# Neighbour sums on padded planes and a root kept in PSUM in the second pass of a two-layer convolution

## The reference, cut to what matters

```python
def reference(x, L0_conv_weights1):        # x: (32, 64, 128, 128) float32
    x = x + _L0_conv_ref(_gn(x), L0_conv_weights1)   # Hartley transform, 20 x 20 modes mixed
    x = x + _L1_conv_ref(_gn(x))                     # layer 1
    return x

def _L1_conv_ref(x):                       # depthwise, 'SAME' padding
    kx = [[-1, 0, 1], [-2, 0, 2], [-1, 0, 1]]
    ky = [[1, 2, 1], [0, 0, 0], [-1, -2, -1]]
    return sqrt(gx * gx + gy * gy + 1e-8)  # gx, gy: x convolved with kx and ky

def _gn(v, G=32, eps=1e-5):                # over pairs of channels of one image
    return (g - mean(g)) / sqrt(var(g) + eps)
```

## Time and profile before

| what | value |
|---|---|
| median of three runs | 2905.59 us (2889.78 to 2907.07) |
| the profiled execution | 2896.12 us, its span 2894.3 us |
| PE busy | 2736.1 us, 95% of the span |
| DVE busy | 2073.9 us, 72% |
| ACT busy | 2096.0 us, 72% |
| POOL busy | 911.3 us, 31% |
| granted TensorE clock over the span | 0.957 |

### The profile page before, as it was taken

How to read it: one execution, slowest core, us unless ns; L and a number is a source line. 1 busy time by engine, 2 the same in 40 slices (tenths; PEclk the granted TensorE clock), 3 DMA queues, 4 the chain that set the end, 5 groups by cost and what they waited for, 6 DMA issues and landing times.

```text
span 2894.3 us, 51534 instructions
## 1 busy us (share of the span) xinstructions
PE 2736.1 (95%) x16764; PEld 2151.0 (74%) x16764; DVE 2073.9 (72%) x2783; ACT 2096.0 (72%) x3633; POOL 911.3 (31%) x533
## 2 busy tenths in 40 slices
PE   6999999999999666899999999999999999999998
PEld 6989889898899666566666666666666666666666
DVE  5767666676777534677877777877777877877777
ACT  5767666576667323578878878878878878888887
POOL 2323233232333302233333333333333333333332
PEclk9999898898999677899999999999999999999999
DMA  6545454454555324155555555555555555555554
GB/s 188 156 133 150 132 146 132 131 155 131 152 144 148 76 62 105 44 150 164 162 152 165 160 150 165 160 156 161 161 153 166 158 152 165 160 153 163 165 167 124
DMA packets 808870, 421.14 MB, mean 146 GB/s; under 512 B 20912, under 2 KB 807344, under 8 KB 807472
## 3 DMA queue, kind: packets, MB, share of 16 engines
q1 hardware_dynamic: 808624, 417.86, 50.7%
HBM read 283.56 MB, written 134.22 MB: 144 GB/s over the span
## 4 chain that ended last, share of the span: by engine, by line
PE 49%; ACT 5%; DVE 3%; issue 3%; DVEq 0%; ACTq 0%
PE g_ps L963 37%; PE y_ps L949 6%; PE v_ps L937 5%; ACT grad L1026 3%; ACT g_ps L1019 2%; DVE coef_t L1063 1%; DVE grad L1075 1%; PE v_ps L925 1%; ACT u_hi L1004 0%; ACT grad L1017 0%; ACT v_sb L1010 0%; DVE xbuf L1100 0%; DVE xbuf L1070 0%; DVE coef L1106 0%; DVEq L1100 0%
## 5 line engine op out<-in xcount | busy, mean ns | idle before, releaser
L963 PE MATMUL g_ps<-u_hi,stencil 128*128 128x512 f32 x2560 | 1054.7, 412 | 1.9 <-DVE grad L1075 1.9
L963 PE MATMUL g_ps<-u_lo,stencil 128*128 128x512 f32 x2560 | 1018.6, 398 | 0.0
L905 POOL TENSOR_TENSOR u_lo<-xbuf,u_hi 128x1024 fp32r<-128x1024 f32 x256 | 565.6, 2209 | 1139.9 <-ACT u_hi L1004 1133.8
L963 PEld LDWEIGHTS g_ps<-u_hi,stencil 128*128 128x128 f32 x2560 | 484.2, 189 | 305.6 <-issue 188.9
L1100 DVE SCALAR_TENSOR_TENSOR xbuf<-xbuf,rows,grad 128x256 f32<-128x256 f32 x1024 | 575.7, 602 | 153.0 <-ACT grad L1026 152.8
L332 PEld LDWEIGHTS t_ps<-first_sb,xbuf 128*128 128x128 f32 x4096 | 525.1, 201 | 68.8 <-issue 42.5
L963 PEld LDWEIGHTS g_ps<-u_lo,stencil 128*128 128x128 f32 x2560 | 482.5, 188 | 103.0
L332 PE MATMUL t_ps<-first_sb,xbuf 128*128 128x64 f32 x4096 | 512.4, 281 | 39.9 <-DMA second_sb<-second 23.5
L1026 ACT ACTIVATE grad<-grad,eps,rows 128x256 f32<-128x256 f32 x1024 | 530.5, 595 | 0.1
L1017 ACT ACTIVATE grad<-g_ps 128x512 f32<-128x512 f32 x512 | 302.2, 590 | 293.1 <-PE g_ps L963 293.0
L1075 DVE TENSOR_TENSOR grad<-grad,g_ps 128x512 f32<-128x512 f32 x512 | 352.0, 687 | 224.6 <-ACT g_ps L1019 218.0
(11 more groups left out here) (116 smaller groups left out, 2383.3 us busy)
## 6 DMA issues: line engine op xcount, KB each, us to landing
xbuf<-x SPq DMA_DIRECT2D x256, 512.0 KB, 5.1
xbuf<-x SPq DMA_DIRECT2D x512, 256.0 KB, 3.0
out<-xbuf SPq DMA_DIRECT2D x512, 256.0 KB, 2.7
xbuf<-weights SPq DMA_DIRECT2D x8, 800.0 KB, 11.2
wmix<-weights SPq DMA_DIRECT2D x8, 800.0 KB, 13.8
second_sb<-second SPq DMA_DIRECT2D x1, 1230.0 KB, 8.4
mats_sb<-mats SPq DMA_DIRECT2D x1, 704.0 KB, 6.5
first_sb<-first SPq DMA_DIRECT2D x1, 32.0 KB, 6.4
```

The source lines that it names most:

```text
L905: nc.gpsimd.tensor_tensor(u_lo[:, r % 2, :, 1:W + 1], x_of(xbuf, r), u_hi[:, r % 2, :, 1:W + 1].bitcast(FP32), ALU.subtract)\
L963: mm = nc.tensor.matmul(g_ps[h][:, axis], stencil[:, m, :], u[:, r % 2, 4 * h:4 * h + 4, o:o + W], start=n == 0, stop=n == len(todo) - 1)
```

## The change

The input buffer gets a second view, `xpad`: eight slots of eight planes, each row of a plane with a zero column on either side (130 columns). The old view, `xbuf`, lies on the same memory and serves the first two stages. With the planes padded:

- POOL `neighbours` computes `pairs`, the sum of each column and the next (129 columns), for step r+2. ACT `high` rounds `pairs` to p_hi, and POOL `low` takes the remainder p_lo from `pairs`. `pairs` has one buffer.
- The filter along the columns is the smoothed difference of two neighbour sums, and the one along the rows the difference of two neighbour sums added. So `sobel` has four taps for each axis and half: 16 a step, for 20 before.
- ACT `squares` puts bank 0's square into `across` in SBUF. DVE `add` writes the sum into bank 1 of g_ps[h], `roots` works in place there, and `finish` reads the root from there. `grad` and `eps` are gone; the root's 1e-8 is a constant of the instruction.
- PE's taps of bank 0 wait for the squares of the step before; those of bank 1 wait for `finished[h]` of the step before. `finished` becomes one semaphore per half, and SP stores a half when it is done.
- The order within a step changes on ACT (roots first, then `high` and `copy_v`) and on DVE (both halves of `finish` before `centre`).

```diff
-        xbuf = sb(keep, "xbuf", [128, SLOTS, CHUNK, W])
+        x_all = sb(keep, "xbuf", [128, XSTEPS * HALF * (W + 2)])
+        xbuf = x_all[:, 0:SLOTS * CHUNK * W].rearrange("p (s n w) -> p s n w", s=SLOTS, w=W)
+
+        xpad = x_all[:].rearrange("p (s n w) -> p s n w", s=XSTEPS, w=W + 2)
...
+
+def x_of(xpad, r):
+
+    return xpad[:, r % XSTEPS, :, 1:W + 1]
...
-        u_hi = sb(ctx, "u_hi", [128, 2, HALF, W + 2], FP32R)
-        u_lo = sb(ctx, "u_lo", [128, 2, HALF, W + 2], FP32R)
-        stencil = sb(ctx, "stencil", [128, 4, 128], FP32R)
-        grad = sb(ctx, "grad", [128, 2, 2, 512])
-        eps = sb(ctx, "eps", [128, 1])
+        pairs = sb(ctx, "pairs", [128, HALF, W + 2])
+        p_hi = sb(ctx, "p_hi", [128, 2, HALF, W + 2], FP32R)
+        p_lo = sb(ctx, "p_lo", [128, 2, HALF, W + 2], FP32R)
+        stencil = sb(ctx, "stencil", [128, 3, 128], FP32R)
+        across = sb(ctx, "across", [128, 2, 512])
...
                 done = sp.snap(t * PSTEPS + r + 1)
-                sp.wait_ge(finished, done)
                 for q in range(2):
-                    sp.dma_start(out_p[:, planes_of(t, r, q), :], x_of(xbuf, r % XSTEPS)[:, 4 * q:4 * q + 4, :])\
+                    sp.wait_ge(finished[q], done)
+                    sp.dma_start(out_p[:, planes_of(t, r, q), :], x_of(xpad, r % XSTEPS)[:, 4 * q:4 * q + 4, :])\
                         .then_inc(stored[r % XSTEPS], 16)
...
-            for part in (u_hi, u_lo):
-                nc.gpsimd.memset(part[:, :, :, 0:W + 2:W + 1].bitcast(FP32), 0.0).then_inc(cleared, 1)
+            nc.gpsimd.memset(xpad[:, :, :, 0:W + 2:W + 1], 0.0).then_inc(padded, 1)
+
+            def neighbours(i, r):
+                pool.wait_ge(centred, at(i, r) + 1)
+                plane = xpad[:, r % XSTEPS]
+                nc.gpsimd.tensor_tensor(pairs[:, :, 0:W + 1], plane[:, :, 0:W + 1], plane[:, :, 1:W + 2],
+                                        ALU.add).then_inc(paired, 1)
 
             def low(i, r):
                 pool.wait_ge(hi_ready, at(i, r) + 1)
-                if not before(i, r, 2):
-                    pool.wait_ge(pe_grad, at(i, r) * 2 - 2)
-                nc.gpsimd.tensor_tensor(u_lo[:, r % 2, :, 1:W + 1], x_of(xbuf, r),
-                                        u_hi[:, r % 2, :, 1:W + 1].bitcast(FP32), ALU.subtract)\
-                    .then_inc(lo_ready, 1)
+                nc.gpsimd.tensor_tensor(p_lo[:, r % 2, :, 0:W + 1], pairs[:, :, 0:W + 1],
+                                        p_hi[:, r % 2, :, 0:W + 1].bitcast(FP32), ALU.subtract).then_inc(lo_ready, 1)
 
             def step(i, r):
                 if not beyond(i, r + 1):
                     low(i, r + 1)
-
+                if not beyond(i, r + 2):
+                    pool.wait_ge(lo_ready, at(i, r) + 2)
+                    neighbours(i, r + 2)
+
+            pool.wait_ge(padded, 1)
+            neighbours(0, 0)
             low(0, 0)
+            pool.wait_ge(lo_ready, 1)
+            neighbours(0, 1)
...
                     pe.wait_ge(lo_ready, at(i, r) + 1)
-                if not before(i, r, 1):
-                    pe.wait_ge(added, at(i, r) * 2 + h - 1)
-
-                SMOOTH, SMOOTH_NEG, DIFF, DIFF_TWICE = range(4)
-                taps = [[(SMOOTH_NEG, 0), (SMOOTH, 2)], [(DIFF, 0), (DIFF_TWICE, 1), (DIFF, 2)]]
+
+                SMOOTH, SMOOTH_NEG, DIFF = range(3)
+                taps = [[(SMOOTH_NEG, 0), (SMOOTH, 1)], [(DIFF, 0), (DIFF, 1)]]
                 for axis in range(2):
-                    todo = [(u, m, o) for m, o in taps[axis] for u in (u_hi, u_lo)]
-                    for n, (u, m, o) in enumerate(todo):
+                    if not before(i, r, 1):
+                        if axis == 0:
+                            pe.wait_ge(squared, at(i, r) * 2 + h - 1)
+                        else:
+                            pe.wait_ge(finished[h], at(i, r))
+                    todo = [(p, m, o) for m, o in taps[axis] for p in (p_hi, p_lo)]
+                    for n, (p, m, o) in enumerate(todo):
                         mm = nc.tensor.matmul(g_ps[h][:, axis], stencil[:, m, :],
-                                              u[:, r % 2, 4 * h:4 * h + 4, o:o + W],
+                                              p[:, r % 2, 4 * h:4 * h + 4, o:o + W],
                                               start=n == 0, stop=n == len(todo) - 1)
                 mm.then_inc(pe_grad, 1)
 
...
             def high(i, r):
-                act.wait_ge(centred, at(i, r) + 1)
+                act.wait_ge(paired, at(i, r) + 1)
                 if not before(i, r, 2):
                     act.wait_ge(pe_grad, at(i, r) * 2 - 2)
-                nc.scalar.activation(u_hi[:, r % 2, :, 1:W + 1], x_of(xbuf, r), ACT.Copy).then_inc(hi_ready, 1)
+                nc.scalar.activation(p_hi[:, r % 2, :, 0:W + 1], pairs[:, :, 0:W + 1], ACT.Copy).then_inc(hi_ready, 1)
...
                 act.wait_ge(pe_grad, at(i, r) * 2 + h + 1)
-                if not before(i, r, 2):
-                    act.wait_ge(finished, at(i, r) - 1)
-                nc.scalar.activation(grad[:, r % 2, h], g_ps[h][:, 0].rearrange("p n w -> p (n w)"), ACT.Square)
-                across = g_ps[h][:, 1].rearrange("p n w -> p (n w)")
-                nc.scalar.activation(across, across, ACT.Square).then_inc(squared, 1)
+                if not before(i, r, 1):
+                    act.wait_ge(added, at(i, r) * 2 + h - 1)
+                nc.scalar.activation(across[:, h], g_ps[h][:, 0].rearrange("p n w -> p (n w)"), ACT.Square)
+                down = g_ps[h][:, 1].rearrange("p n w -> p (n w)")
+                nc.scalar.activation(down, down, ACT.Square).then_inc(squared, 1)
 
             def roots(i, r, h):
                 act.wait_ge(added, at(i, r) * 2 + h + 1)
                 inv_var = rows[:, 0].rearrange("p t n -> p (t n)")
                 for k in range(2):
-                    f = grad[:, r % 2, h, 256 * k:256 * (k + 1)]
-                    a = nc.scalar.activation(f, f, ACT.Sqrt, bias=eps[:],
+                    f = g_ps[h][:, 1, 2 * k:2 * k + 2]
+                    a = nc.scalar.activation(f, f, ACT.Sqrt, bias=EPS_SOBEL,
                                              scale=inv_var[:, bass.ds(group_planes(i, r, h, k), 1)])
                 a.then_inc(rooted, 1)
 
@@ -1038,13 +1053,13 @@
             high(0, 0)
 
             def step(i, r):
+                if not before(i, r, 1):
+                    roots(i, r - 1, 0)
+                    roots(i, r - 1, 1)
                 if not beyond(i, r + 1):
                     high(i, r + 1)
                 if not beyond(i, r + 3):
                     copy_v(i, r + 3)
-                if not before(i, r, 1):
-                    roots(i, r - 1, 0)
-                    roots(i, r - 1, 1)
                 squares(i, r, 0)
                 squares(i, r, 1)
...
-                f = grad[:, r % 2, h]
-                V.tensor_tensor(f, f, g_ps[h][:, 1].rearrange("p n w -> p (n w)"), ALU.add).then_inc(added, 1)
+                down = g_ps[h][:, 1].rearrange("p n w -> p (n w)")
+                V.tensor_tensor(down, across[:, h], down, ALU.add).then_inc(added, 1)
...
                 dve.wait_ge(rooted, at(i, r) * 2 + h + 1)
                 for k in range(2):
-                    xs = x_of(xbuf, r)[:, 4 * h + 2 * k:4 * h + 2 * k + 2, :].rearrange("p n w -> p (n w)")
-                    v = V.scalar_tensor_tensor(
-                        xs, xs, mean[:, bass.ds(group_planes(i, r, h, k), 1)],
-                        grad[:, r % 2, h, 256 * k:256 * (k + 1)], ALU.add, ALU.add)
-                if h == 1:
-                    v.then_inc(finished, 1)
+                    xs = x_of(xpad, r)[:, 4 * h + 2 * k:4 * h + 2 * k + 2, :]
+                    v = V.scalar_tensor_tensor(xs, xs, mean[:, bass.ds(group_planes(i, r, h, k), 1)],
+                                               g_ps[h][:, 1, 2 * k:2 * k + 2], ALU.add, ALU.add)
+                v.then_inc(finished[h], 1)
...
-                V.tensor_copy(stencil[:, n, :], mat(m))
-            V.tensor_scalar(stencil[:, 3, :], mat("diff"), 2.0, None, ALU.mult)
-            V.memset(eps[:], EPS_SOBEL).then_inc(setup, 1)
+                copied = V.tensor_copy(stencil[:, n, :], mat(m))
+            copied.then_inc(setup, 1)
...
                 if not before(i, r, 1):
                     add(i, r - 1, 1)
+                    finish(i, r - 1, 0)
+                    finish(i, r - 1, 1)
                 if not beyond(i, r + 2):
                     centre(i, r + 2)
                 if 1 <= s <= COEF_STEPS and not beyond(i, r - s + PSTEPS):
                     for part in range(4 // COEF_STEPS * (s - 1), 4 // COEF_STEPS * s):
                         for q in range(2):
                             coefficients(pair_of(i, r) + 1, part, q)
-                if not before(i, r, 1):
-                    finish(i, r - 1, 0)
                 add(i, r, 0)
                 if group(i, r) is not None:
```

(2 more changed lines are left out.)

28 lines of the change are left out of this document (13 added, 15 removed).

## The result

| | median us | runs |
|---|---|---|
| before | 2905.59 | 13 |
| changed | 2885.46 | 13 |

The ratio of the two is 0.994, with a 95% interval of 0.9919 to 0.9961. One run on each side was disturbed (5479 and 3795 us): the medians stand over all 13, the ratio leaves the two out. The changed kernel is 20 us faster, a small difference but clear of the noise; 24 us slower was forecast. The profiled execution took 2890.3 us, the one of before 2896.1.

A forecast was written before the change was run, and what follows sets the result against it. TensorE bounds the kernel before; afterwards the loop through the banks should set plain steps. Terms -49 + 69 - 10 + 14 = +24 us on the median 2905.6 gave 2930 us, range 2845 to 2995 (a tenth left out at either end).

The forecast's parts named there:

- the root: ScalarE's square root of 256 elements: 0.48 to 0.50 us, following by 0.40; bounds 0.36 and 0.595 us.
- Taps and bound: Sobel on TensorE, 20 taps to 16: its step falls 0.94 us to 5.48 us and stops being the bound.
- The loop through the banks: Plain step, squares, two roots, two additions, twelve taps: 6.11 us against 6.42, -49 us over 157 intervals.
- The second loop: Through the single buffer `pairs`, remainder, neighbour sum, rounding: 5.8 us, hidden 0.3 us deep.
- The coefficient steps: 28 steps where VectorE and GpSimd take turns, so TENSOR_SCALARs wait: 8.9 us against 6.42, +69 us.
- The clock: TensorE falls to 1.2 GHz once or twice in each of seven coefficient stretches: +14 us, bounds 0 and +50.
- theory (b): Experiments' theory: in coefficient steps VectorE and GpSimd take turns; this delay and the following clock falls take the gain back.
- The transpose steps: 70 steps with fewer taps but a wait for `copy_coef`: 7.0 us against 7.2, -10 us in all.
- Rival 1: Turn taking costs little, coefficient step near 6.4 us, clock stays: -59 us, 2847 us; chance 0.20.
- Rival 2: TensorE's clock does not hold in plain steps either: +105 us on top, 3035 us; chance 0.10.
- Rival 3: Neighbour sum longer than remainder, +125 us, or root keeps 0.595 us, +40, 2970 us; chance 0.20 together.
- a loss of 83 against a gain of 59: Second pass: coefficient steps +69 and clock +14 us against plain steps -49 and transpose steps -10; sum +24 us, slower.

The follow-up runs named there:

- the experiment: Changed kernel with the root's bias read from a column in SBUF again instead of the constant: 2931.5 us, ratio 1.0095 to the kernel before.
- the sums alone: Changed kernel with padded planes, GpSimd neighbour sums and 16 taps kept, but gradient sum and root in SBUF, order and bank release as before: 3076.7 us.
- the banks alone: Kernel before, 20 taps and padding kept, with sum, root and addition in PSUM, constant bias, banks held and new order: 3017.1 us, ratio 1.037.

## Why the prediction was wrong

The order of things was as forecast. What failed are three terms of the sum, all in the same direction: the period of a coefficient step (8.9 us taken, 8.1 measured; in it the neighbour sum, 2.23 against 1.91, and the roots), the root (0.50 taken, 0.443 measured) and the price of the clock's falls (14 us taken, about 2 measured). The measured parts of the pass sum to -25.5 us where mine summed to +24.

**Taps and bound.** Right. TensorE's 5.48 us did not become the bound, and the chain shows what did.

**The loop through the banks.** Right in its order, forecast 6.11 and measured 6.00. The step that failed is the root: 0.48 to 0.50 us taken, following by 0.40, against 0.443 and 0.355. I allowed for the column, which is worth 91 ns by the experiment, but put the move from SBUF to PSUM at nothing for the root, though I had named it as unseen for the addition. It is worth 61 ns a root. Over the 150 plain intervals this and the rest of the pass's plain steps make -16 us of the error (46.5 forecast at 0.31 each, 62.6 measured). The Trainium skill, "ScalarE: Activation LUTs", section "What ACT_TABLE_LOAD costs", has 93 ns for a column, and the trace agrees. The Trainium skill, "Perfetto Trace Analysis", section "Optimizing Scalar/DVE Operations", gives ScalarE some 93 ns of access overhead on SBUF and 51 on PSUM as busy time, 42 apart, and says that a profiled duration holds about twice that; the 61 measured lie between 42 and 84.

**The second loop.** Named rightly as hidden, wrongly priced: the remainder took 2.43 (2.23 taken), the neighbour sum 1.91 (2.23 taken). Two reads of the same tile, one shifted, and a plain fp32 result are not the price of a subtraction rounded to fp32r; that they were was an assumption from "same engine, operation and size".

**The coefficient steps.** The mechanism was the forecast one and decided the case. The four lines of TENSOR_SCALAR average 1.76 to 1.88 us, inside my 1.5 to 2.3. The period was 8.9 and is 8.10. Piece by piece for the step shown above, measured against taken: remainder 2.40 (2.23), gap before the neighbour sum 0.16 (0.23, for the first TENSOR_SCALAR), neighbour sum 1.91 (2.23), rest of the second TENSOR_SCALAR 0.23 (0.23), addition 0.67 (0.69), release 0.14 (0.14), four roots 1.44 (1.70), rounding 1.08 (1.05), release 0.08 (0.17). These sum to 8.1 against 8.7, and I had then gone up to 8.9 for grants that would need the full 0.42 us. The neighbour sum and the roots are 0.58 of it. 28 steps x 0.8 = 22 us of the error: the largest piece.

**The clock.** The falls were forecast rightly, their price was not. The clock held in plain steps and fell one to three times in each of the seven stretches. But the five intervals of a set take 39.1 to 39.2 us in the first, the fourth and the sixth pair, with two, one and one falls in them, and that is just four steps of 8.07 and the first transpose interval, 6.86: the falls cost nothing there. In the second and the seventh pair 0.6 and 1.6 us are left. TensorE is not what these steps wait for, which would explain it; that is argued, not shown. The third and the fifth pair take 4.4 us more each. There the loop is re-entered, and the kernel with the scaling moved takes 4.7 and 4.3 us more in the same places; the kernel before took 1.1 and 0.5. So the falls cost about 2 us, which is -12 of the error; of theory (b) the delay stands and the falls hardly count. The re-entries, which I had not in the sum, are +7. The interval that I counted as plain in each set was a transpose one (eleven a set, 77 and not 70) and gained nothing: +2.

**The transpose steps.** -0.26 us each instead of -0.15, -8 us of the error, and the reason was wrong. The wait for `copy_coef` was not in the loop (the swap of the axes gained nothing). The wait for `copy_v` ahead of the transposes and the transposes themselves were (moving them gained 0.6 us a step). With this the pieces of the error are -16, -22, -12, +7, +2 and -8: together -49, as between +24 and -25.5.

**The rivals.** Rival 1 asked for TENSOR_SCALARs under 0.8 us; they took 1.76 to 1.88, so the turns did cost. Its 2847 would have needed what the moved scaling did, and that gave 2816. The measured 2885 lies halfway between this rival and the forecast, but the mechanism was the forecast's. Rival 2 fell: between 1700 and 1820 us TensorE idled 6.3 of 120 us, a third of a microsecond in each step, and the granted clock was 1.00. The rule of the Trainium skill, "TensorE: Matmul & The Clock Gate", section "A second HAM failure mode: psum-queue depth-cycling", does not show in this kernel's plain steps. Rival 3's root that keeps its column costs +46 us where I had +40, but with a root of 534 ns and not 595. The direction went wrong because I set a loss of 83 against a gain of 59, and the runs gave 55 against 81. The root's size lay inside its bounds, toward the end that I had not taken; the neighbour sum had an upper bound in rival 3 and none below the remainder's own time, and that is what the working lacked.

## What to carry to other kernels

While GpSimd is busy with operations on SBUF, count for VectorE an operation of the kinds below whose tensors all lie in SBUF as waiting for the end of GpSimd's running one, however small it is; put it into the gap in which GpSimd waits, or bring an operand into PSUM. When a buffer's release closes a loop over several engines, only what stands between the release and the loop's last work counts: moving the transposes out of it gained 0.6 us a step without making them shorter, and no busy share shows that. And where a forecast is the small difference of two large terms, price the operations whose memory or inputs change one by one, since their errors can all point one way.

## What the runs showed of the hardware

- VectorE and GpSimd: TENSOR_SCALAR, TENSOR_TENSOR, SCALAR_TENSOR_TENSOR and COPY took turns with GpSimd when all their tensors lay in SBUF (TENSOR_SCALAR 0.42 us unhindered and up to 2.15 in the changed kernel, COPY 0.16 and 1.87, SCALAR_TENSOR_TENSOR 0.44 to 0.48 and up to 2.72 in the sums alone; TENSOR_TENSOR was only seen hindered, 1.67 to 2.40). With the root in PSUM SCALAR_TENSOR_TENSOR did not: all 1024 of L1115 in the changed kernel take 472 to 485 ns. The Trainium skill, "SBUF — State Buffer", section "SBUF: two separate sides", names an exclusive lock between GpSimd and VectorE operations in a two-port mode, or with two SBUF inputs against a GpSimd operation that reads SBUF. These runs agree, with the numbers above; in which mode TENSOR_SCALAR and COPY ran no row shows.
- ScalarE, root of 256 elements: 443 ns in PSUM with one column, 534 in PSUM with two, 595 in SBUF with two, and 502 in SBUF with one (the sums alone). A root of 512 in PSUM with one column takes 656.
- GpSimd: 1032 elements a lane take 1.91 us as an fp32 sum and 2.43 as a subtraction to fp32r, in the changed kernel.
- Plain steps take 5.90 us instead of 6.00 in the last 63 steps, which stand behind the program's loop and wait on constants instead of computed counts; no operation's mean differs by more than 4 ns there, so the 0.1 us lies between operations. With the banks alone the same two are 6.84 and 6.96; in the kernel before both are 6.41. That it is the computed counts was not tested.
- Open: why the untouched first part ends 20 us earlier or later from one profiled execution to the next, and why an interval takes 7.4 to 11.4 us where the program's loop is re-entered (7.8 and 7.2 in the kernel before).
